# Cross-attention with a gated low-rank block on one core: small VectorE steps in other quarters, GpSimd's front pair first, and another bank table

## The reference

```python
x = x + xattn(LN(x), ctx, ctx)      # 32 query heads, 8 key heads, head size 32; k and v are the same context
x = x + ffn(LN(x), ...)             # 8 experts: squared projections, a sigmoid gate, the best expert's
                                    # rank-8 update and bias, mixed with x by the gate
# xattn: scores = einsum('bkgsd,bktd->bkgst', qh, kh) / sqrt(32); softmax over t; einsum with vh
```

## Time and profile before

| | us |
|---|---|
| median of 3 runs | 1023.92 |
| lowest, highest | 1020.99, 1025.22 |
| the profiled execution | 1022.49 |
| its span, first to last instruction | 1020.7 |
| mean granted TensorE clock | 0.995 |

### The profile page before, as it was taken

How to read it: one execution, slowest core, us unless ns; L and a number is a source line. 1 busy time by engine, 2 the same in 40 slices (tenths; PEclk the granted TensorE clock), 3 DMA queues, 4 the chain that set the end, 5 groups by cost and what they waited for, 6 DMA issues and landing times.

```text
span 1020.7 us, 24586 instructions
## 1 busy us (share of the span) xinstructions
PE 947.1 (93%) x9518; PEld 371.1 (36%) x9518; DVE 902.3 (88%) x1106; ACT 730.8 (72%) x1301; POOL 801.6 (79%) x454
## 2 busy tenths in 40 slices
PE   4789999999999999999999999999999999999996
PEld 3223333333333333333333323333222225777773
DVE  6979999999999999999999999998888886888976
ACT  5367788888888888888888877888777777554440
POOL 6259999999999999999999999999999998222110
PEclk9999999999999999999999999999999999999998
DMA  8674776767676767676867685756655744766423
GB/s 246 191 172 109 165 169 155 166 152 169 149 169 154 173 145 176 142 171 148 184 142 179 132 192 129 182 121 153 121 119 138 163 93 147 246 209 233 159 104 164
DMA packets 319875, 164.18 MB, mean 161 GB/s; under 512 B 182216, under 2 KB 307240, under 8 KB 319760
## 3 DMA queue, kind: packets, MB, share of 16 engines
q1 hardware_dynamic: 319456, 161.76, 64.3%
q0 software_dynamic: 304, 0.85, 0.4%
HBM read 107.58 MB, written 54.53 MB: 159 GB/s over the span
## 4 chain that ended last, share of the span: by engine, by line
PE 35%; DVE 31%; issue 25%; ACT 5%; POOL 3%; DMA 1%; SPq 0%; DVEq 0%; POOLq 0%; ACTq 0%
DVE row_max L927 14%; PE psum L590 8%; PE psum L604 6%; PE psum L617 5%; PE psum L735 5%; DVE den_t L939 4%; PE psum L552 4%; ACT probs L864 3%; PE psum L713 3%; DVE o_t L933 3%; DVE probs L1138 2%; PE psum L578 2%; DVE prod_mem L985 2%; PE psum L701 1%; ACT prod_mem L817 1%
## 5 line engine op out<-in xcount | busy, mean ns | idle before, releaser
L864 ACT ACTIVATE probs<-psum 128x512 f32<-128x512 f32 x1024 | 554.7, 596 | 131.0 <-PE psum L590 113.0
L927 DVE TENSOR_REDUCE row_max<-psum 128x4 f32<-128x2048 f32 x248 | 565.8, 2281 | 64.3 <-PE psum L552 64.0
L590 PE MATMUL psum<-q_stack,k_stack 97*32 97x512 f16 x4096 | 334.8, 386 | 9.9 <-issue 3.5
L365 POOL TENSOR_TENSOR sums<-probs 128x2048 f32<-128x2048 f32 x63 | 287.7, 4566 | 17.5 <-ACT probs L864 17.4
L353 POOL TENSOR_TENSOR sums<-probs 128x2048 f32<-128x2048 f32 x63 | 287.2, 4559 | 7.1 <-PE psum L627 5.5
L604 PE MATMUL psum<-probs,v_in 128*32 128x512 f32 x2048 | 268.8, 598 | 1.0
L590 PEld LDWEIGHTS psum<-q_stack,k_stack 97*32 97x32 f16 x4096 | 96.7, 95 | 258.8 <-ACT probs L864 149.2
L552 PE MATMUL psum<-high_mem 32*128 32x512 f16 x992 | 98.0, 384 | 23.7 <-DVE row_max L927 20.1
L325 POOL TENSOR_TENSOR o_t<-o_t,inv 128x512 f32<-128x512 f32 x64 | 67.2, 1049 | 40.7 <-DVE inv L945 38.8
L330 POOL TENSOR_TENSOR o_all<-o_all,o_t 128x512 f32<-128x512 f32 x64 | 81.6, 1274 | 9.2
L604 PEld LDWEIGHTS psum<-probs,v_in 128*32 128x32 f32 x2048 | 59.2, 110 | 60.9 <-issue 16.2
(11 more groups left out here) (119 smaller groups left out, 759.2 us busy)
## 6 DMA issues: line engine op xcount, KB each, us to landing
q_stack<-q_split SPq DMA_DIRECT2D x192, 128.0 KB, 3.4
xa<-in_x_dram SPq DMA_DIRECT2D x32, 512.0 KB, 4.7
o_all<-in_x_dram SPq DMA_DIRECT2D x256, 64.0 KB, 2.4
x_attended<-o_all SPq DMA_DIRECT2D x64, 256.0 KB, 4.1
out_dram<-probs SPq DMA_DIRECT2D x32, 512.0 KB, 2.9
q_split<-prod_mem SPq DMA_DIRECT2D x15, 1024.0 KB, 5.3
xa<-x_attended SPq DMA_DIRECT2D x16, 512.0 KB, 4.5
probs<-x_attended SPq DMA_DIRECT2D x16, 512.0 KB, 4.7
```

Source lines behind the costliest of these rows:

```text
L365: pool.tensor_tensor(sums[:, 2 * u % SUMS], probs[:, u % 2, 0], probs[:, u % 2, 1], ALU.add).then_inc(front_done, 1)
L590: last = pe.matmul(st_ps[row:row + D, bank_of["score", u, n], :], k_stack[:, u % SLOTS, t * P + row:t * P + row + D], q_stack[:, u % SLOTS ...
L864: act.activation(probs[:, s, keys, g, :], st_ps[:, bank_of["score", u, n], :], ACT.Exp, scale=EXP_SCALE).then_inc(exped, 1)
L927: dve.reduce_max(row_max[:, u % 2, t:G * ST:ST], s_ps[:], AX.X).then_inc(reduced, 1)
```

## The change

Four things. On VectorE, the denominators of an even unit are transposed a quarter later (second instead of first), their inverse a quarter later (third), the second half of the moments in the third quarter of an even unit, and variance and guard in the third and fourth quarter of the odd unit. On GpSimd, in an even unit the front pair's sum stands ahead of `normalise`, and the inverse root comes last. The bank table reckons in quarters: each use has a time at which it starts, and a bank is free 0.4 quarters after a score or a maximum, 0.6 after a piece, and at a fixed quarter for denominators, where it counted places in the list before.

```diff
+            QUARTERS_KEPT = {"score": 0.4, "max": 0.4, "part": 0.6}
+            DEN_TAKEN_AT = (ST + 2.0, 3.95)
+            filled = [(-LEAD, ("part", n, i)) for n in range(FIRST) for i in range(PIECES)]
...
-            KEPT = {"score": 2, "max": 2, "den": (5, 5), "part": 6}
...
-                kept = KEPT["den"][use[1] % 2] if use[0] == "den" else KEPT[use[0]]
-                free_at[bank], last_in[bank] = max(i, free_at[bank]) + kept + 1, use
+                if use[0] == "den":
+                    free_at[bank] = (use[1] + 1) * ST + DEN_TAKEN_AT[use[1] % 2]
+                else:
+                    free_at[bank] = max(at, free_at[bank]) + QUARTERS_KEPT[use[0]]
+                last_in[bank] = use
...
-                    if live(u - 2):
+                    if live(u - 2) and u % 2 == 1:
                         normalise(u - 2)
-                    if u % 2 == 1 and whole(tile_of(u) + 1):
-                        inverse_root(tile_of(u) + 1)
                     if 0 <= u < UNITS - 1:
...
+                    if live(u - 2) and u % 2 == 0:
+                        normalise(u - 2)
+                    if u % 2 == 1 and whole(tile_of(u) + 1):
+                        inverse_root(tile_of(u) + 1)
...
-                        if t == 0 and live(u - 2) and u % 2 == 0:
-                            take_denominators(u - 2)
...
-                        if t == 1 and live(u - 2):
+                        if t == 1 and live(u - 2) and u % 2 == 0:
+                            take_denominators(u - 2)
+                        if t == (2 if u % 2 == 0 else 1) and live(u - 2):
                             invert(u - 2)
...
-                        if early and t == 1:
+                        if early and t == 2:
                             last_moments(n + 1)
-                        if early and t == 2:
+                        if late and live(u) and whole(n + 1) and t == 2:
                             variance(n + 1)
+                        if late and live(u) and whole(n + 1) and t == ST - 1:
                             guard(n + 1)
```

More of the change, by code:

```diff
@@ L199, in xattn_ffn @@
             DOWN_AT, FOLD_AT = ((-AHEAD, ST - 1), (1 - AHEAD, 0)), (1 - AHEAD, ST - 1)
-            filled = [("part", n, i) for n in range(FIRST) for i in range(PIECES)]
+            QUARTERS_KEPT = {"score": 0.4, "max": 0.4, "part": 0.6}
+            DEN_TAKEN_AT = (ST + 2.0, 3.95)
+            filled = [(-LEAD, ("part", n, i)) for n in range(FIRST) for i in range(PIECES)]
             for u in range(-AHEAD, UNITS + 2):
@@ L205, in xattn_ffn @@
                     half = MIDST[u % 2][t] - BEGIN[u % 2][t]
+                    now = []
                     if u % 2 == 1 and t < PIECES and whole(tile_of(u)):
-                        filled.append(("part", tile_of(u), t))
-                    filled += scores[:half]
+                        now.append(("part", tile_of(u), t))
+                    now += scores[:half]
                     if t == 2 and live(u + 1):
-                        filled.append(("max", u + 1, 0))
-                    filled += scores[half:]
+                        now.append(("max", u + 1, 0))
+                    now += scores[half:]
                     if t == (ST - 1 if u % 2 == 1 else 2) and live(u - 1):
-                        filled.append(("den", u - 1, 0))
-            KEPT = {"score": 2, "max": 2, "den": (5, 5), "part": 6}
-            bank_of, bank_before, free_at, last_in = {}, {}, [0] * BANKS, [None] * BANKS
-            for i, use in enumerate(filled):
+                        now.append(("den", u - 1, 0))
+                    filled += [(u * ST + t + (i + 1) / (len(now) + 1), use) for i, use in enumerate(now)]
+            bank_of, bank_before, free_at, last_in = {}, {}, [-LEAD] * BANKS, [None] * BANKS
+            for i, (at, use) in enumerate(filled):
                 bank = min(range(BANKS), key=lambda b: free_at[b])
```

## The result

The changed kernel takes 1075.36 us (median of 4 runs, 1073.83 to 1077.16); the kernel before, run on the same chip, takes 1024.57. The ratio is 1.0503, with an interval of 1.047 to 1.0535: five per cent slower, where 1070 us were forecast. Its profiled execution took 1076.41 us, of which 1074.6 is the span.

A forecast was written before the change was run, and what follows sets the result against it. Bound: a cycle in which TensorE's row matmuls wait for VectorE's maximum to read the banks, and the next maximum for them. 1022.5 us plus 38.5 (odd units), 10.2 (even units), -1 (first unit) gave 1070; range 1054 to 1083.

The forecast's parts named there:

- The odd unit: Odd units with an input tile: scores waiting in the pieces' bank lengthen three quarters by 0.35, 0.82 and 0.31, together 1.48 us.
- the overlap rival: Of an odd unit's three bank waits only the longest counts, 0.82 us: 1053 us in all; chance 0.08.
- The third quarter: Odd unit: score 11 waits for low part 2, 3.75 us; piece 2 behind exp 7 gives 3.73; 0.31 longer.
- what would show it: Signs in the later profile: pair about 27.1 us, scores' weight loads waiting for VectorE's low parts about 0.7 us each.
- The even unit: Scores 4 to 8 share two banks, each behind an earlier exp, so an even unit takes 0.33 us longer.
- the 0.24: Even unit, first quarter: moving one of VectorE's two transposes away lets the next maximum start 0.24 us earlier.
- Unit 0: First unit: scores 1 to 11 get three banks instead of two, -1 us, between 0 and -2.4.
- GpSimd: Its new order costs and gains 0, with 1.9 us of room before VectorE's o_t transpose needs the normalisation.
- VectorE's moves in the ring: Steps moved between quarters of the repeating VectorE-TensorE cycle cost 0; without idle cover at most 0.40 us an odd unit.
- the tail 0: The end of the kernel adds nothing, since only the names of banks differ there.
- The bounds: Limits on forecast terms: forecast alone 1061 to 1080 us; whole range 1054 to 1083, its top for hand-overs 0.1 dearer.
- The rule on the queue: TensorE pulling weight loads ahead of waits would save 8 us, giving 1062; the profile row said nothing is saved.

The follow-up runs named there:

- the kept bank: Changed kernel, but in odd units no score up to 12 and no row maxima enter the bank of a tile's pieces while these are under way: 1039.43 us.
- the table alone: Kernel before with only the new computation of the banks, VectorE's and GpSimd's steps left where they were: 1069.62 us, ratio 1.0461.
- score 3 alone: Changed kernel with the pieces' bank held for the pieces, except that score 3 of odd units may take it: 1056.74 us in a single execution.
- score 7 alone: Changed kernel with the pieces' bank held for the pieces, except that score 7 of odd units may take it: 1078.88 us in a single execution.
- the step put back: Changed kernel, but in the pass after the last unit VectorE takes unit 62's denominators ahead of unit 63's rows again: 1069.79 us, ratio 1.0462.
- the repeat: The kernel with only score 7 of odd units allowed in the held pieces' bank, run again four times against the kernel before: 1080.91 us, ratio 1.0563.

## Why the prediction was right, and where it was not

**The odd unit** went as said: quarters of 3.45, 3.79 and 3.72 where 3.51, 3.75 and 3.75 were worked out, 1.42 us longer where the sum had 1.48. The hand-over from VectorE's step to the waiting load measured 0.05 to 0.06 us where 0.12 had been read from the earlier trace rows; the second quarter took 0.52 from the load of M to R in place of 0.45, which makes up for it. That the scores in the chain are the cause is shown by the kept bank, which takes 35.0 us of span away, and by the table alone, which brings the pair to 27.06. That scores 3 and 7 each count is shown by score 3 alone at +0.70 a pair (26.33 to 25.63) and score 7 alone at +1.1 (26.72 to 25.63, in the pairs at full clock). The two together would be 1.8, and the chain with all three costs 1.42, so the waits do overlap in part; the overlap rival as it was put, with only the longest counted, would have had a pair of about 26.5 in the changed kernel, not 27.05.

The third quarter came out at its size for the second of the two reasons given. The prediction put score 11's wait for low part 2 first (3.75) and piece 2 behind exp 7 "nearly as late" (3.73). With score 7 alone in the bank, score 11 has no such wait and the quarter takes 3.72 all the same, so piece 2 accounts for all of it and score 11 for nothing. Nor do the scores wait "about 0.7 us each", as was said under what would show it: the loads of scores 3, 7 and 11 wait 1.15, 0.62 and 0.20, TensorE itself 0.74 and 0.28 at the first two.

**The even unit** came out 0.30 longer, 0.33 being forecast. The load of score 8 went at R + 5.81 (433.67 less 427.86), where the chain of exps gave 5.83. The 0.33 itself does not come out of the working: that gives 0.27 at the third R (411.57 less 411.30) and at most 0.36 at the row matmuls (411.12 less 410.76), and what was measured is 0.31 at the third R and 0.30 over the unit. And the reasoning had a flaw that the size hides: the 0.33 was said to stand "with the 0.24 taken off", and the 0.24 of an earlier first quarter was never in the chain. That chain starts at exps, not at the maximum. The table alone, without the early quarter, is as long. The bound "0.57 longer if the early R brings nothing" was therefore wrong: it brought nothing, and the unit took 0.30.

**Unit 0** gave 1.22 us (its third maximum starts at 51.69, where it was 52.91), 1 being forecast. In the two kernels with the old table that maximum starts at 52.9 and 53.5, in the eight with a new one at 51.1 to 52.8, so the direction is likely. But two executions of one kernel, the one with score 7, lie 1.55 apart (51.23 and 52.78), so that the size here agrees is luck as much as reckoning.

**GpSimd** at nothing was right: 0.9997 alone, and in the changed kernel its normalisation ends at 441.19 (439.92 + 1.27), 2.05 us before VectorE asks for it, where 1.9 had been reckoned.

**VectorE's moves in the ring** at nothing were right too: the pair is 27.06 without them and 27.05 with them.

**The step that failed** is the one that says "the tail 0, since there only the names of banks differ". The tail cost 9.1 us. One of the moved steps, the denominators' transpose, is also issued in the pass behind the last unit, and there it changed places with the step that waits some 4 us for GpSimd. In the ring this exchange is harmless; at the seam TensorE has nothing else to do, idles 5.65 us, and then works at half clock for a further 6.8: against the kernel before, the projection starts 5.7 us later (27.9 for 22.2 after the last maximum) and takes 1.9 longer, which is 7.6 of the 9.1; how the rest comes about was not followed up. The table alone (tail 187.3) shows that the banks' names have no part in it, and the step put back (188.3) that the place of this step has nearly all, 8.5 of 9.1 us. A step moved by a quarter has to be followed into the passes in which the units around it are missing. In span the forecast was 6.2 us too low (47.7 for 53.9): the ring was taken 2.9 too long and the tail 9.1 too short. That the two errors go against each other, and bring the median within 5.4 us, is luck.

**The bounds.** Two of them do not follow from the terms given for them. An even term of 0.1 with an odd one of 1.3 gives 1058 us, not 1061, as the lower end of the forecast alone; and hand-overs 0.1 dearer, at 1.8 an odd unit, give 1078.5, not 1083. The measured time lies within the bounds either way.

**The rule on the queue.** In the load queue's rows above, score 3's load stands idle for 1.15 us and starts, with its matmul, 0.06 after the low part; it was not pulled ahead, and the pair is 0.09 below the forecast one (27.05 for 27.14), not 0.3. The estimate of 1062 us that went by the Trainium skill ("TensorE: Matmul & The Clock Gate", section "Architectural detail: the array is 16× 32×32, not 1× 128×128") did not come true; in these rows a load that is itself behind a wait is where the wait is paid.

## What to carry to other kernels

When a table hands out shared banks by estimated release times, look at each new pair of neighbours in a bank and ask what is queued behind the one that waits: on an engine that takes its queue in order, a bank that comes free late delays everything behind it (0.74 us of TensorE's time at score 3 here), and the next user of the bank waits once more (0.47 us at piece 1). A step moved one slot along a loop is moved in the first and the last passes too; draw those out by hand, since the neighbours that covered it are missing there. And a gain in one quarter of a ring is only a gain if the longest chain of the next quarter begins at it: here it began at exps, and 0.24 us an even unit went nowhere.

## What was not expected of the hardware

TensorE's granted clock fell to its lower level, 1.2 GHz of 2.4, after waits that look small. At the seam it stood near half (0.51) over 6.8 us, after 5.65 us of idle. With score 7 alone in the pieces' bank, it fell after one wait of 1.05 us and one of 0.47 shortly behind it, in 10 of 25 pairs in one run and 9 in another, and each fall took the third quarter from 3.72 to 5.05 or more and the pair from 26.72 to 27.84 or more. The changed kernel has more waits, but none as long: 0.74 and 0.47 at score 3 and piece 1, 0.28 and 0.47 at score 7 and piece 2, in every odd unit. Each of its third quarters in the 25 pairs takes 3.72 or 3.73. So removing two of the three scores from the chain made the kernel slower (1080.91 against 1075.36 us, ratios of 1.0563 and 1.0503 whose intervals stand apart). It is the clock: what the nine pairs of the repeat take above 26.72 adds up to 11.7 us, and without it the estimate is 1069. What decides between a pair that falls and one that doesn't, with waits alike to 0.01 us, no run here shows.
